# A half group's gathered results added late in the batch ahead of its own, and the first half of the values evacuated by ScalarE, in an attention stage that VectorE and TensorE share

## The chip, the cores and the metric

The kernel runs on one core of a Trainium2 chip. The metric is the time of one execution on the device, in microseconds (us). Before the change it is 1008.19 us, the median of 3 runs (1007.99 to 1009.01).

In what follows PE is TensorE, DVE is VectorE, ACT is ScalarE, POOL is GpSimd and SP is SyncE. PSUM is the memory that PE writes to, eight banks of 512 float32 columns on 128 partitions. SBUF is the working memory.

## The reference

The kernel computes a transformer of eight stages on `x` of shape (8, 256, 128): each stage adds, scaled by a gate, an attention or an expert network of the normed `x`. The change touches the seam of stages 2 and 3. Stage 2 is a network of experts that works on tokens sorted by expert, so each token's two results must be gathered back and added. Stage 3 is self-attention with 16 heads of 8 channels over the 256 tokens of a batch and 64 context tokens:

```python
x = x + jnp.tanh(g_ffn[0])   * _L0_ffn_ref(_layernorm(x), ...)          # stage 2: experts
x = x + jnp.tanh(g_xattn[1]) * _L1_xattn_ref(_layernorm(x), ctx, ...)   # stage 3: "Heads"
# stage 3, per batch of 256 tokens and per head:
#   P = softmax(q k^T / sqrt(8)) over 256 tokens + 64 context tokens;  out = (P v) W_proj + b_proj
```

Tokens of stage 3 must be normed, so a batch can be projected only once stage 2's results for it have been added to `x` and its statistics are known.

## The kernel before

Each engine runs its own list of instructions, in an order that the program writes out by hand. Engines meet only at semaphores. So the order on each engine is fixed, and what can change is who waits for whom.

The stage (class `HeadsStage`, lines 1160 to 1757) handles 8 batches. Its loop on PE, DVE and ACT runs through 10 rounds of 20 steps. In step n of round b:

- PE computes one bank of scores, 128 queries by 512 keys (L1385, or L1390 for the context keys in every fifth step), into one of three banks.
- DVE reduces that bank to row maxima (L1670). PE may not start the scores of step n before DVE has done step n - 3.
- PE computes, 16 steps behind, one bank of transposed scores (L1405, L1410), and ACT exponentiates it (L1590). PE may not be more than two such banks ahead of ACT.
- `extras(b, at)`, called with the step `at` from 0 to 19 on each of the three engines, adds the rest of the pipeline at fixed steps: for batch b + 1 the projection and the laying out of queries and keys, for batch b - 1 the products with the values, and for batch b - 2 the output projection and its addition to `x`.

The pieces that matter here:

- **The sums over values.** PE writes them for two groups of four heads into bank 5 (L1428, L1431, function `values`). When half a batch is complete, the bank is copied to the SBUF tile `AT` (L1691, function `evacuate`), PE transposes `AT` (L1440, function `turn_parts`), and DVE divides (L1677, L1684, function `take_parts`). The second half of batch b - 2 is copied at step 0 of round b, the first half of batch b - 1 at step 10. PE transposes at steps 1 and 11. Both copies are DVE's. The text calls them the **last copy** and the **first copy**. In the first copy the data are ready long before: PE writes them at steps 7 and 8.
- **The keys of the next batch.** DVE's masking copies (L1659, function `mask`) at steps 12 and 13 follow PE's transposes of the keys at step 11. PE's transposes of the second half of the queries (L1342, step 14) go into the same bank, so they wait for both masking copies. The text calls this point the **mask point** of a round.
- **The results of stage 2.** POOL gathers them from memory for each half group (256 tokens, the tokens of one batch) by indirect DMA (L997), four per half group. DVE adds them to `x` with four sums (L938, L940) and computes statistics (L154, L157), function `add_results`. POOL turns the statistics to a scale (L233, L236), and DVE norms at step 14 (L168). In round b, `add_results` for half group b + 2 stands at step 5, for b from 0 to 5. The text calls this block of eight DVE instructions the **added block**.
- **POOL** splits the queries and keys of batch b + 1 into bf16 parts during the first half of round b (L1218, L1226, L1231, L1233), then gathers the second pair of results of half group b + 3, then waits for PE (step 16) and splits the context keys of batch b + 2 (L1257, L1218, L1226 on 64 partitions), copies context values (L1269) and adds a bias (L1291).

Of the kernel before, what the change touches and what calls it, by code (L numbers as in the profile page):

```python
# [17 lines left out]
ACT = mybir.ActivationFunctionType  # L18
# [8 lines left out]
NG = NT // GROUP  # L27
# [91 lines left out]
class Norm:  # L119
# [122 lines left out]
    def act(self, a):  # L242
        self.turn.act(a)
# [916 lines left out]
class HeadsStage:  # L1160
# [379 lines left out]
    def act(self, a):  # L1540
        c, s = self.c, self.s
        bank = c.bank

        def split(b, k):
            a.wait_ge(s["qkv"], 2 * b + 1)
            if b:
                a.wait_ge(s["k_rows"], b)
            rows = bank[k][:, :].rearrange("p (i n h c) -> p n i h c", i=2, n=2, c=8)
            for n in range(2):
                a.activation(self.rest[:, n].rearrange("p (i h) c -> p i h c", i=2), rows[:, n], ACT.Copy,  # L1550
                             scale=1.0 if n else self.SCALE).then_inc(s["split"], 1)

        def split_values(b, k):
            a.wait_ge(s["qkv"], 2 * b + 2)
            if b >= 3:
                a.wait_ge(s["av"], 4 * (b - 2))
            a.activation(self.V[:, b % 3, :, 0:144].rearrange("p i (h c) -> p i h c", c=9)[:, :, :, 0:8],
                         bank[k][:, 0:2 * D].rearrange("p (i h c) -> p i h c", i=2, c=8), ACT.Copy) \
                .then_inc(s["split"], 1)

        def mask_context(b, k):
            a.wait_ge(s["k_t"], 3 * b + 2)
            for q in range(2):
                a.activation(self.KM[b % 2][:, q:16:2, S:S + SC],
                             bank[k].bitcast(BF16)[:, 0:512].rearrange("p (k t) -> p k t", t=SC), ACT.Copy,
                             scale=c.parity[:, q:q + 1]).then_inc(s["masked"], 1)

        def mask(b, g, q, k, done):
            a.wait_ge(s["k_t"], 3 * b + (3 if g else 1))
            a.activation(self.KM[b % 2][:, 8 * g + q:8 * g + 8:2, 0:S],  # L1570
                         bank[k].bitcast(BF16)[:, :].rearrange("p (k t) -> p k t", t=S), ACT.Copy,
                         scale=c.parity[:, q:q + 1]).then_inc(done, 1)

        def copy_again(b, g, k):
            a.wait_ge(s["q_top"], 2 * b + g + 1)
            a.activation(self.QE[:, 4 * g:4 * g + 4, :],  # L1576
                         bank[k].bitcast(BF16)[:, :].rearrange("p (k t) -> p k t", t=S), ACT.Copy) \
                .then_inc(s["q_again"], 1)

        def copy_out(b):  # L1580
            a.wait_ge(s["o_t"], b + 1)
            a.activation(self.OT, bank[6][:, 0:S], ACT.Copy).then_inc(s["o_turned"], 1)

        def exponentials(e):
            b, j, k = e // 20, e // 5 % 4, e % 5
            a.wait_ge(s["st"], e + 1)
            if 4 * b + j >= 2 and k in (0, 4):
                a.wait_ge(s["av"], 4 * b + j - 1)
            out = self.prob[(4 * j + k) % 8] if k < 4 else self.prob_c[:, j % 2, :]
            a.activation(out, bank[3 + e % 2][:, :], ACT.Exp).then_inc(s["exp"], 1)  # L1590

        def extras(b, at):
            ahead, behind, late = b + 1 < B, 0 <= b - 1 < B, 0 <= b - 2 < B
            if at == 2 and ahead:
                split(b + 1, 7)
            if at == 4:
                if ahead:
                    split_values(b + 1, 6)
                if behind:
                    copy_again(b - 1, 1, 7)  # L1600
            if at == 6 and late:
                copy_out(b - 2)
            if at == 14 and b < B:
                copy_again(b, 0, 6)
            if at == 17 and ahead:
                mask_context(b + 1, 6)
            if at == 19 and b + 2 < 2 * NG:
                turns.act_halves(a, b + 2, 1)
            if at in (18, 19) and ahead:
                mask(b + 1, 1, at - 18, 7, s["masked"])  # L1610

        turns = self.norm.turn
        turns.act_halves(a, 0, 1)
        a.wait_ge(s["ones_set"], 1)
        split(0, 0)
        split_values(0, 1)
        for q in range(2):
            mask(0, 0, q, 3, s["masked_v"])
        mask_context(0, 5)
        for q in range(2):  # L1620
            mask(0, 1, q, 4, s["masked"])
        turns.act_halves(a, 1, 1)
        for n in range(self.STEP * (B + 2)):
            if 0 <= n - self.LAG < self.STEP * B:
                exponentials(n - self.LAG)
            extras(n // self.STEP, n % self.STEP)

    def dve(self, v):
        c, s = self.c, self.s
        bank, own = c.bank, c.dve_chain  # L1630

        def next_stats(b):

            if b % 2 and self.next is not None:
                v.wait_ge(s["added"], 2 * b + 2)
                self.next.norm.stats(v, b // 2)

        def split_maxima(b, g, part):

            top, top_c = self.top[:, :, 8 * g:8 * g + 8], self.top_c[:, :, 8 * g:8 * g + 8]  # L1640
            rows = self.Q[b % 2][:, :, :, :].rearrange("p (i h) s c -> p i h (s c)", i=2)[:, :, 8 * g:8 * g + 8, :]
            if part == 0:
                v.wait_ge(s["maxed"], 20 * b + 10 * g + 10)
                own.link(v, v.tensor_tensor(top, top, top_c, ALU.min))
                own.link(v, v.tensor_copy(rows[:, :, :, 48], top))
                own.link(v, v.tensor_tensor(top, top, rows[:, :, :, 48], ALU.subtract))
            else:
                own.link(v, v.tensor_copy(rows[:, :, :, 49], top))
                own.link(v, v.tensor_tensor(top, top, rows[:, :, :, 49], ALU.subtract))
                v.tensor_copy(rows[:, :, :, 50], top).then_inc(s["top_rows"], 1)  # L1650
# [33 lines left out]
                v.tensor_tensor(self.O[:, :, at:at + 32].rearrange("p i (r k) -> p i r k", r=4), parts[:, :, :, 0:8],  # L1684
                                bc(rz[:, :, :, None], (P, 2, 4, 8)), ALU.mult).then_inc(s["heads"], 1)

        def evacuate(b, half):
            v.wait_ge(s["av"], 4 * b + 2 * half + 2)
            if b or half:
                v.wait_ge(s["parts"], 2 * b + half)  # L1690
            v.tensor_copy(self.AT, bank[5][:, :]).then_inc(s["evac"], 1)  # L1691

        def add(b):
            v.wait_ge(s["product"], b + 1)
            v.wait_ge(s["biased"], b + 1)
            for i in range(2):
                j = 2 * b + i
                v.scalar_tensor_tensor(c.X[:, j, :], bank[6][:, S + i * P:S + (i + 1) * P],
                                       c.gates[:, 1:2], c.X[:, j, :], ALU.mult, ALU.add).then_inc(s["added"], 1)

        def extras(b, at):
            ahead, behind, late = b + 1 < B, 0 <= b - 1 < B, 0 <= b - 2 < B
            if at == 0:
                if late:
                    evacuate(b - 2, 1)
                if behind:
                    split_maxima(b - 1, 1, 0)
            if at == 1 and behind:
                split_maxima(b - 1, 1, 1)
            if at == 2 and late:  # L1710
                take_parts(b - 2, 1)
            if at == 8 and late:
                add(b - 2)
            if at == 9 and ahead:
                copy_queries(b + 1, 0, 7)
            if at == 10:
                if behind:
                    evacuate(b - 1, 0)
                if b < B:
                    split_maxima(b, 0, 0)  # L1720
            if at == 11 and b < B:
                split_maxima(b, 0, 1)
            if at == 12:
                if behind:
                    take_parts(b - 1, 0)
                if ahead:
                    mask(b + 1, 0, 7)
            if at == 13 and ahead:
                mask(b + 1, 1, 7)
            if at == 15 and ahead:  # L1730
                copy_queries(b + 1, 1, 7)
            if at == 17 and 3 <= b - 2 < B - 1:
                next_stats(b - 2)
            if at == 14 and b == 5:
                next_stats(1)
            half = b + 2
            if half < 2 * NG:
                if at == 5:
                    self.before.add_results(v, half)
                if at == 14:  # L1740
                    self.norm.normalize(v, half // 2, half % 2)

        v.wait_ge(s["ones_set"], 1)
        v.wait_ge(s["split"], 1)
# [1570 lines left out]
```

## Time and profile before

| what | value |
|---|---|
| median of 3 runs | 1008.19 us (1007.99 to 1009.01) |
| the profiled execution: its own time | 1002.98 us |
| the profiled execution: span | 1001.3 us |
| PE, DVE, ACT, POOL busy | 79%, 65%, 38%, 37% of the span |
| mean granted clock of PE | 0.902 of full speed |
| the stage's steps in the trace | about 215 to 447 us |

The profiled execution is 5.21 us shorter than the median of the plain runs, so differences are worked out inside the trace and then applied to the median. A row of the timeline reads: start in us, duration in us, engine, line, operation, output and input, count, and in brackets the idle time of the engine just before, with what ended it. Consecutive instructions of one line are merged into one row; the last instruction of one row can overlap the first of the next by some hundredths, since the engines are pipelined.

Round b begins at step 0, whose last copy is easy to find in the trace. It starts at 270.31 us in round 2, 325.12 us in round 4, 352.52 us in round 5, 380.05 us in round 6 and 406.92 us in round 7. Rounds 2 to 4 are equal to 0.01 us.

### The profile page before, as it was taken

The numbers are of one execution on the slowest core, as the hardware profiler recorded it, in microseconds if no ns is written. First come the engines' busy times: TensorE is split into PE (matmuls) and PEld (weight loads), VectorE is DVE, ScalarE is ACT, GpSimd is POOL, SyncE is SP. The second block draws the span as 40 slices with busy tenths as digits, with TensorE's granted clock in tenths as the row PEclk, the third lists the DMA queues.
The fourth block names the chain that finished last, engine by engine and source line by source line (L and its number), as shares of the span: only waits on it lengthen the run. The fifth ranks groups of instructions, "written<-read, shape, count | busy, mean of one in ns | idle before, by whom it ended". The sixth has DMA issues, their size and how long they took to land.

```text
span 1001.3 us, 14752 instructions
## 1 busy us (share of the span) xinstructions
PE 791.5 (79%) x5059; PEld 540.7 (54%) x5059; DVE 650.8 (65%) x1844; ACT 376.6 (38%) x735; POOL 366.1 (37%) x502
## 2 busy tenths in 40 slices
PE   3635999646888888888989899888799879984374
PEld 1624888433444444433469666567343647774263
DVE  4774222366888888746977678996467458977421
ACT  2122444234666666751522564442200234441210
POOL 5234433276565535007745101102001015453353
PEclk9857999867999999998999899997899889995597
DMA  8605777200000000000000000000000230002210
GB/s 206 235 11 163 213 212 203 62 19 14 12 10 9 12 1 2 2 1 0 1 1 1 1 1 1 1 1 1 1 0 0 64 106 1 1 2 84 79 56 27
DMA packets 51772, 45.46 MB, mean 45 GB/s; under 512 B 6804, under 2 KB 47655, under 8 KB 51442
## 3 DMA queue, kind: packets, MB, share of 16 engines
q1 hardware_dynamic: 48146, 36.91, 12.5%
q0 software_dynamic: 3552, 7.61, 2.9%
q8 instruction: 41, 0.67, 0.3%
q14 instruction: 33, 0.27, 0.1%
HBM read 36.90 MB, written 7.80 MB: 45 GB/s over the span
## 4 chain that ended last, share of the span: by engine, by line
PE 53%; DVE 29%; issue 7%; POOL 4%; ACT 3%; DMA 3%; POOLq 0%; SPq 0%; DVEq 0%; ACTq 0%
PE psum L2473 6%; DVE scratch L1670 4%; PE psum L1131 4%; PE psum L2068 3%; PE psum L2747 3%; PE psum L2777 3%; DVE stats L154 3%; DVE XN L168 2%; PE psum L1428 2%; PE psum L610 2%; PE psum L277 2%; PE psum L1142 2%; DVE XN L1972 2%; PE psum L2113 2%; PE psum L2765 1%
## 5 line engine op out<-in xcount | busy, mean ns | idle before, releaser
L1670 DVE TENSOR_REDUCE scratch<-psum 128x2 f32<-128x512 f32 (+1 forms) x160 | 105.8, 683 | 35.3 <-PE psum L1390 19.3
L1590 ACT ACTIVATE scratch<-psum 128x512 f32<-128x512 f32 x160 | 93.9, 602 | 71.6 <-PE psum L1405 63.9
L233 POOL TENSOR_SCALAR veps<-moments 128x4 f32<-128x4 f32 (+1 forms) x48 | 10.4, 217 | 293.9 <-DVE moments L157 292.7
L277 PE MATMUL psum<-ident,XN 128*128 128x128 f32 x144 | 31.0, 352 | 44.8 <-DVE XN L168 41.2
L903 DVE SCALAR_TENSOR_TENSOR scratch<-psum,b_block_bias,scratch 128x256 f32<-128x256 f32 (+1 forms) x48 | 18.6, 430 | 71.9 <-ACT scratch L1056 64.0
L975 POOL DMA_INDIRECT scratch<-pair_rows,b_gather_at x39 | 39.3, 1007 | 68.6 <-PE psum L1104 41.8
L2473 PE MATMUL psum<-late,scratch 128*128 128x512 f32 x128 | 57.0, 607 | 5.7 <-DVE routing_wide L2416 5.0
L2679 POOL TENSOR_TENSOR scratch<-scratch,arena 128x1024 f32<-128x1024 f32 x16 | 30.4, 1902 | 76.9 <-DVE arena L2897 76.9
L1405 PE MATMUL psum<-scratch,arena 128*128 128x256 bf16 x256 | 49.3, 274 | 5.6 <-ACT scratch L1576 4.4
L292 ACT ACTIVATE XT<-psum 128x512 f32<-128x512 f32 (+1 forms) x40 | 22.2, 560 | 83.7 <-PE psum L277 83.6
L236 POOL TENSOR_TENSOR rstd<-veps,minus_half 128x4 f32<-128x4 f32 (+1 forms) x48 | 48.5, 1010 | 6.7 <-POOL veps L233 0.2
L277 PEld LDWEIGHTS psum<-ident,XN 128*128 128x128 f32 x144 | 21.3, 182 | 53.3 <-issue 25.9
L1385 PE MATMUL psum<-arena 128*128 128x512 bf16 x128 | 49.5, 393 | 0.6 <-DVE scratch L1670 0.6
L2473 PEld LDWEIGHTS psum<-late,scratch 128*128 128x128 f32 x128 | 24.8, 195 | 37.2 <-issue 30.5
L997 POOL DMA_INDIRECT arena<-pair_results,b_slot_bits x32 | 33.4, 1043 | 28.8 <-DMA pair_results<-scratch 21.0
L2427 DVE SCALAR_TENSOR_TENSOR X<-psum,routing_wide,X 128x128 f32<-128x128 f32 x128 | 33.8, 341 | 14.8 <-PE psum L2473 14.8
L1131 PE MATMUL psum<-scratch,arena 128*128 128x256 f32 (+1 forms) x192 | 39.5, 349 | 3.5 <-DVE scratch L903 2.8
L1972 DVE SCALAR_TENSOR_TENSOR XN<-psum,routing_wide,XN 128x128 f32<-128x128 f32 x128 | 35.4, 342 | 10.6 <-PE psum L2113 10.6
L2113 PEld LDWEIGHTS psum<-late,scratch 128*128 128x128 f32 x256 | 33.2, 191 | 16.3 <-issue 15.5
L1218 POOL CAST scratch<-scratch 64x384 bf16<-64x384 f32 (+3 forms) x64 | 32.3, 504 | 18.2 <-PE psum L1342 14.3
L168 DVE TENSOR_SCALAR XN<-X,moments,rstd 128x128 f32<-128x128 f32 x128 | 35.3, 338 | 5.3 <-POOL rstd L236 5.2
L1342 PE MATMUL psum<-ident,scratch 128*128 128x128 bf16 (+1 forms) x320 | 24.7, 224 | 16.0 <-POOL scratch L1277 7.5
(453 smaller groups left out, 2050.7 us busy)
## 6 DMA issues: line engine op xcount, KB each, us to landing
arena<-in_L_ffn_w SPq DMA_DIRECT2D x72, 128.0 KB
arena<-in_L_ffn_wg SPq DMA_DIRECT2D x24, 256.0 KB
wide<-in_L_xattn_Wkv SPq DMA_DIRECT2D x1, 2048.0 KB
wide<-in_L_ffn_W SPq DMA_DIRECT2D x1, 2048.0 KB, 8.8
late<-in_L_ffn_W SPq DMA_DIRECT2D x8, 256.0 KB, 6.9
pair_results<-scratch SPq DMA_DIRECT2D x15, 128.0 KB
X<-in_x SPq DMA_DIRECT2D x2, 512.0 KB, 5.0
C<-in_ctx SPq DMA_DIRECT2D x2, 512.0 KB, 6.8
```

What stands on the lines that cost most here:

```text
L168: v.tensor_scalar(self.dst[:, j, :], self.src[:, j, :], c.moments[:, j, 0:1], c.rstd[:, j:j + 1], ALU.subtract, ALU.mult).then_inc(c.norme ...
L236: g_.tensor_tensor(c.rstd[:, a:b], c.veps[:, a:b], c.minus_half[:, a:b], ALU.pow).then_inc(c.rstd_done, (b - a) // 2)
L277: last = t.transpose(c.bank[self.banks[g % 2]][:, i * P:(i + 1) * P], self.src[:, j, :], c.ident[:])
L975: g.indirect_dma_start(self.rows[:, u, i, :], None, self.given, bass.IndirectOffsetOnAxis(ap=self.gather_at[:, at:at + 1], axis=0), bounds ...
L1131: last = t.matmul(c.bank[4 + n % 2][:, k * self.SLOTS:k * self.SLOTS + rows], self.wg[:, n % self.RING, q, k * P:(k + 1) * P], self.z[:, n ...
L1385: last = t.matmul(out[:, 0:2 * S], queries[:, 4 * g + k, i * P:(i + 1) * P], keys[:, h:h + 2, 0:S], start=True, stop=True)
L1405: last = t.matmul(out[:, n * S:(n + 1) * S], keys[:, h, n * P:(n + 1) * P], self.QE[:, h // 2, :], start=True, stop=True)
L1590: a.activation(out, bank[3 + e % 2][:, :], ACT.Exp).then_inc(s["exp"], 1)
L1670: v.tensor_reduce(out, bank[m % 3][:, :].rearrange("p (h t) -> p h t", t=n), AX.X, ALU.max, negate=True).then_inc(s["maxed"], 1)
L1972: v.scalar_tensor_tensor(c.XN[:, j, :], c.bank[2 + n % 2][:, i * D:(i + 1) * D], one[:, j, e:e + 1], c.XN[:, j, :], ALU.mult, ALU.add) \
L2113: last = t.matmul(c.bank[2 + n % 2][:, i * D:(i + 1) * D], self.hidden[:, n % 2, i * P:(i + 1) * P], self.w2[:, e, :], start=True, stop=True)
L2473: last = t.matmul(c.bank[4 - 4 * (q % 2) + 2 * i + half][:, :], self.hidden[:, k, j * P:(j + 1) * P], self.w_down[:, k, half * 512:(half + ...
```

## The change

Two moves. First, `add_results` leaves step 5. Half group 2 stays there in round 0; half groups 3 to 7 are now added at step 17 of rounds 0 to 4, that is one round earlier and late in it. Normalization stays at step 14. Second, the first copy leaves DVE's step 10 and becomes an activation (L1588 in the new numbering) on ACT, at the same step, behind the exponentials of that step. The last copy stays with DVE. The number of copies, sums and statistics doesn't change.

```diff
 (ACT)
+        def evacuate_first(b):
+            a.wait_ge(s["av"], 4 * b + 2)
+            if b:
+                a.wait_ge(s["parts"], 2 * b)
+            a.activation(self.AT, bank[5][:, :], ACT.Copy).then_inc(s["evac"], 1)
...
+            if at == 10 and behind:
+                evacuate_first(b - 1)
 (DVE)
-        def evacuate(b, half):
-            v.wait_ge(s["av"], 4 * b + 2 * half + 2)
-            if b or half:
-                v.wait_ge(s["parts"], 2 * b + half)
+        def evacuate_last(b):
+            v.wait_ge(s["av"], 4 * b + 4)
+            v.wait_ge(s["parts"], 2 * b + 1)
             v.tensor_copy(self.AT, bank[5][:, :]).then_inc(s["evac"], 1)
...
-                if behind:
-                    evacuate(b - 1, 0)
...
+            if at == 5 and b == 0:
+                self.before.add_results(v, 2)
+            if at == 17 and b + 3 < 2 * NG:
+                self.before.add_results(v, b + 3)
             half = b + 2
-            if half < 2 * NG:
-                if at == 5:
-                    self.before.add_results(v, half)
-                if at == 14:
-                    self.norm.normalize(v, half // 2, half % 2)
+            if at == 14 and half < 2 * NG:
+                self.norm.normalize(v, half // 2, half % 2)
```

On DVE, in the kernel before, from the maxima of step 17 of round 1 to the first copy of round 2 (the maxima are L1670, the last and the first copy both L1691, the block L938 to L157):

```order
259 L1670 TENSOR_REDUCE scratch<-psum 128x2 x3
260 L1670 TENSOR_REDUCE scratch<-psum 128x8
261 L1670 TENSOR_REDUCE scratch<-psum 128x2
262 L1691 COPY scratch<-psum 128x512
...
274 L1670 TENSOR_REDUCE scratch<-psum 128x8
275 L1670 TENSOR_REDUCE scratch<-psum 128x2
276 L938 SCALAR_TENSOR_TENSOR X<-arena,routing_small,X 128x128
277 L940 SCALAR_TENSOR_TENSOR X<-arena,routing_small,X 128x128
...
286 L1670 TENSOR_REDUCE scratch<-psum 128x2
287 L1691 COPY scratch<-psum 128x512
```

The same place in the changed kernel, where the maxima are L1678 and the last copy is L1698:

```order
258 L1678 TENSOR_REDUCE scratch<-psum 128x2 x2
259 L938 SCALAR_TENSOR_TENSOR X<-arena,routing_small,X 128x128
260 L940 SCALAR_TENSOR_TENSOR X<-arena,routing_small,X 128x128
261 L938 SCALAR_TENSOR_TENSOR X<-arena,routing_small,X 128x128
262 L940 SCALAR_TENSOR_TENSOR X<-arena,routing_small,X 128x128
263 L154 BN_STATS stats<-X 128x6 x2
264 L157 BN_AGGR moments<-stats 128x2 x2
265 L1678 TENSOR_REDUCE scratch<-psum 128x2
266 L1678 TENSOR_REDUCE scratch<-psum 128x8
267 L1678 TENSOR_REDUCE scratch<-psum 128x2
268 L1698 COPY scratch<-psum 128x512
```

The block now stands three maxima ahead of the last copy, and neither the block nor the first copy stands between the last copy and the mask point any more.

On ACT, before, eight exponentials stand in a row in the middle of a round:

```order
121 L1590 ACTIVATE scratch<-psum 128x512 x2
122 L1582 ACTIVATE scratch<-psum 128x256
123 L1590 ACTIVATE scratch<-psum 128x512 x8
124 L1576 ACTIVATE scratch<-psum 128x1024
```

In the changed kernel the first copy (L1588) stands in the middle of the eight, which are L1596 there:

```order
123 L1596 ACTIVATE scratch<-psum 128x512 x2
124 L1582 ACTIVATE scratch<-psum 128x256
125 L1596 ACTIVATE scratch<-psum 128x512 x4
126 L1588 ACTIVATE scratch<-psum 128x512
127 L1596 ACTIVATE scratch<-psum 128x512 x4
128 L1576 ACTIVATE scratch<-psum 128x1024
```

The first copy is behind the exponentials of step 10 and ahead of those of step 11. The orders of PE and POOL are as before.

## Rows read from the trace of the kernel before

**Rows 1.** Windows of rounds 4 and 6, steps 0 to 10: length, busy by engine.

```profile
325.10:339.80 14.70, 12.59 (x124) 6.85 (x122) 12.68 (x32) 9.67 (x19) 9.48 (x17) 1.00 0.04 10
380.05:394.50 14.45, 12.44 (x123) 6.85 (x122) 9.96 (x25) 9.44 (x18) 7.24 (x15) 1.00 0.01 1
```

**Rows 2.** The copies' line L1691: who waited for it (us, times).

```profile
  PE psum L1440: 15.0, 15
```

**Rows 3.** Chain of what ended last, within round 4: start, us, what.

```profile
335.11 0.49 DVE stats L154 x2
...
339.90 0.60 DVE scratch L1691
...
345.42 0.62 PE psum L1342 x8
```

**Rows 4.** Timeline of DVE, round 4.

```profile
325.12 0.68 DVE L1691 COPY scratch<-psum 128x512 f32<-128x512 f32 x1
...
332.54 0.65 DVE L938 SCALAR_TENSOR_TENSOR X<-arena,routing_small,X 128x128 f32<-128x128 f32 x1
...
333.79 0.83 DVE L938 SCALAR_TENSOR_TENSOR X<-arena,routing_small,X 128x128 f32<-128x128 f32 x1
...
335.74 1.85 DVE L1670 TENSOR_REDUCE scratch<-psum 128x2 f32<-128x512 f32 x3
...
344.62 0.74 DVE L1659 TENSOR_SCALAR arena<-psum,parity 128x1024 bf16<-128x1024 bf16 x1
...
347.59 1.27 DVE L1670 TENSOR_REDUCE scratch<-psum 128x2 f32<-128x512 f32 x2
...
352.52 0.68 DVE L1691 COPY scratch<-psum 128x512 f32<-128x512 f32 x1
```

**Rows 5.** Timeline of PE, round 4, step 11.

```profile
340.64 0.63 PE L1440 MATMUL psum<-ident,scratch 128*128 128x128 f32 x4 [1.63 <-DVE scratch L1691]
```

**Rows 6.** Timeline of ACT, round 4, steps 9 to 11.

```profile
337.96 1.69 ACT L1590 ACTIVATE scratch<-psum 128x512 f32<-128x512 f32 x3 [0.97 <-PE psum L1405]
```

**Rows 7.** Timeline of DVE, round 6.

```profile
380.05 0.68 DVE L1691 COPY scratch<-psum 128x512 f32<-128x512 f32 x1
...
399.29 0.74 DVE L1659 TENSOR_SCALAR arena<-psum,parity 128x1024 bf16<-128x1024 bf16 x1
```

**Rows 8.** Timeline of POOL, round 4.

```profile
333.80 0.67 POOL L1233 TENSOR_TENSOR scratch<-scratch 128x256 f32<-128x256 f32 x1
...
348.66 0.42 POOL L1226 TENSOR_TENSOR scratch<-scratch 64x128 f32<-64x128 f32 x1
349.14 0.39 POOL L1218 CAST scratch<-scratch 64x256 bf16<-64x256 f32 x1
349.62 0.42 POOL L1226 TENSOR_TENSOR scratch<-scratch 64x128 f32<-64x128 f32 x1
350.10 0.28 POOL L1218 CAST scratch<-scratch 64x128 bf16<-64x128 f32 x1
```

**Rows 9.** The first sums' line L938: duration in ns min/median/max.

```profile
L938 DVE SCALAR_TENSOR_TENSOR X<-arena,routing_small,X x16: 339/648/835, 197.6 to 361.2; 128x128 f32<-128x128 f32 x16
```

**Rows 10.** Timeline of ACT, rounds 7 and 8, from step 9.

```profile
417.66 1.69 ACT L1590 ACTIVATE scratch<-psum 128x512 f32<-128x512 f32 x3 [0.52 <-PE psum L1405]
...
438.83 2.33 ACT L1590 ACTIVATE scratch<-psum 128x512 f32<-128x512 f32 x4 [0.30 <-PE psum L1405]
```

**Rows 11.** Timeline of PE, rounds 7 and 8, step 11.

```profile
419.48 0.63 PE L1440 MATMUL psum<-ident,scratch 128*128 128x128 f32 x4 [0.75 <-DVE scratch L1691]
...
439.72 0.60 PE L1440 MATMUL psum<-ident,scratch 128*128 128x128 f32 x4
```

**Rows 12.** Timeline of DVE, PE and POOL, end of round 0.

```profile
239.52 1.87 DVE L1670 TENSOR_REDUCE scratch<-psum 128x2 f32<-128x512 f32 x3
...
244.60 1.13 PE L1327 MATMUL psum<-c_Wqkv,XT 128*128 128x256 f32 x4 [0.88 <-ACT arena L1570]
...
239.10 0.28 POOL L1257 COPY scratch<-C 64x128 f32<-64x128 f32 x1 [2.25 <-PE psum L1342]
```

More of the change, by code:

```diff
@@ L1704, in extras @@
                 if late:
-                    evacuate(b - 2, 1)
+                    evacuate_last(b - 2)
                 if behind:
```

## Prediction

> **What bounds the stage now.** I read the page first, then windows of half rounds, the chain of what ended last inside one round, and then the timelines of DVE, PE, ACT and POOL around the three places that the change touches.
>
> In steps 0 to 10 of round 4, DVE is busy 12.68 us of 14.70 and PE 12.59, at the full clock. In round 6, which has no added block, DVE is busy only 9.96 us, yet the stretch still lasts 14.45 [rows 1]. So the block's 3.2 us (332.54 to 335.74) [rows 4] are mostly covered where they stand. PE would set the pace of that stretch without them.
>
> The chain inside round 4 shows two regimes. PE leads from the last copy to step 4. Then DVE leads through the block and the first copy up to the mask point. At 345.42 PE's transposes of the queries take over [rows 3], and PE leads up to step 19, when DVE's maxima and the last copy follow. The added block and the first copy both lie on the chain. PE waits 15.0 us in 15 waits for the copies of L1691 [rows 2]; in round 4 it stands idle 1.63 us before the transposes that follow the first copy [rows 5].
>
> I split a round at two points. E is the start of the last copy (325.12 in round 4, next at 352.52). M is the end of the second masking copy, 344.62 + 0.74 = 345.36. So E to M is 20.24 us and M to the next E is 7.16 us [rows 4].
>
> **E to M, rounds 1 to 5: about 0.86 us less each.** The block leaves this stretch, and so does the first copy. Round 6 shows what is left without the block: 399.29 + 0.74 - 380.05 = 19.98 us [rows 7]. The first copy is still in it and stands on the chain with 0.60 [rows 3], so DVE's way is 19.38 us, 0.86 less than 20.24.
>
> PE must be able to follow. ACT's three exponentials of steps 9 to 11 start at 337.96 and take 1.69, some 0.55 apart [rows 6]. The copy comes behind the second. It starts at 339.06, and as one more instruction of that size (128x512 float32 out of PSUM, 0.60 with its tail) it ends at 339.65. PE started its transposes 0.14 after the DVE copy's end (339.82 + 0.68 = 340.50, start 340.64 [rows 3, 5]), so it starts at 339.80 now: 0.84 earlier. PE also had about 0.17 of waiting left at M, by the same gap of issue, so 1.0 is there for PE and DVE's 0.86 decides. The exponentials of step 11 come 0.55 later; PE asks for them only at step 13, two banks on, so that is hidden.
>
> **M to the next E, rounds 1 to 4: about +0.36 us each.** This is where the block goes. Behind M, DVE works without a gap up to the end of step 17's maxima, 347.59 + 1.27 = 348.86 [rows 4], and then waits for PE in steps 18 and 19. The block starts at about 348.8. How long it lasts there is the unknown of this prediction; call it A.
>
> In its old place A is 3.2 us, though its sums can take 0.34 us each (the minimum) and not 0.65 (the median) [rows 9]. Round 4 shows why: the second L938 starts at 333.79 and ends at 334.62, 0.15 behind the end of POOL's 128x256 sum (333.80 + 0.67 = 334.47) [rows 4, 8]. A sum with two SBUF inputs stands until POOL's instruction is through. At the new place POOL is at work too, but with smaller instructions on 64 partitions, ending at 349.08, 349.53, 350.04 and 350.38 [rows 8].
>
> Ending each of the four sums either 0.34 after its start or 0.14 after the POOL instruction that runs, and starting the next a few hundredths on, I get ends at 349.22, 349.67, 349.93 to 350.18, and 350.31 to 350.56. From the last sum's end to the next maxima it takes 0.66 in the old place (statistics start at 335.11, a few hundredths behind the sum, and the maxima at 335.74 [rows 3, 4]), so the next maxima start at 350.97 to 351.22. I take A = 2.3, ending at 351.1. Then steps 18, 19 and 0 run back to back at 0.60, and the next E comes at 352.9. Before, it was 352.52 [rows 4]. The cover was DVE's idle time in steps 18 and 19; what the block needs beyond that cover is the +0.38, and I take 0.36 for A = 2.3 exactly (M + 7.52).
>
> The Trainium skill (SBUF — State Buffer, Who interferes with whom) speaks of an exclusive lock between a VectorE instruction with two SBUF inputs and a GpSimd one that reads SBUF: whoever starts first holds the port pair to its end. The pair of rows at 333.8 agrees in its 0.15 us. The rule speaks against this change, since the block is put among POOL's context-key work rather than into a quiet place. By the worst reading of it, all four sums wait out an instruction as long as the old ones.
>
> Bounds of A from rows: four sums near 0.34 and 0.66 of statistics give 2.0 us; four sums of 0.83, the largest [rows 9], give 4.0 us. My 2.3 is worked out from the POOL rows that really stand there.
>
> **Round 0: nothing.** The block starts there at about 240.7, behind the second of the maxima at 239.52. PE's projection for the next batch at 244.60 waits for ACT's mask [rows 12], not for DVE. Up to A = 2.55 this hides the block (240.7 + A + 0.60 for step 18, then some 0.75 of PE work to the projection); beyond that it costs A - 2.55. The gathers must have landed. POOL itself waits for them in its queue ahead of its copy at 239.10, so they have landed by then [rows 12], 1.6 us ahead of the block.
>
> **Rounds 5 to 8.** Round 5 gains 0.86 and has no block behind M; DVE sets its pace to the end, so it is kept. Round 6 never had a block: the copy's 0.60 goes, and PE's transposes come earlier by a like amount. Round 7 gains nothing: ACT's exponentials there start at 417.66, so the ACT copy would end at 417.66 + 2 x 0.55 + 0.60 = 419.35 and PE start at 419.49, where it starts at 419.48 now [rows 10, 11]. Round 8 loses. PE has no scores there and waits for ACT; at step 11 it starts its transposes at 439.72 without any wait for the copy. ACT's exponentials of steps 9 and 10 start at 438.83 and some 0.55 later, the copy runs from 439.93 to 440.50, PE starts at 440.63 [rows 10, 11]: +0.91 on the chain.
>
> **The sum.** Rounds 1 to 4: 4 x (-0.86 + 0.36) = -2.0. Round 5: -0.86. Round 6: -0.60. Round 8: +0.91. Together -2.55 us, and 4 x (A - 2.3) more for another A. The profiled execution would go from 1002.98 to about 1000.4. It lies 5.2 us under the median of the runs; the rounds of this stage run at the full clock [rows 1], so I apply the difference as it is: 1008.19 - 2.55 = 1005.6 us. What comes after the stage is moved, not changed. Differences below 0.2% (2.0 us) can't be told from no change here, and -2.55 is hardly over that.
>
> **Rivals.**
>
> 1. *The block stays expensive, but not ruinous* (A from 2.43 to 3.26). For it: 3.2 is what every block from round 1 on takes now. Against it: POOL's instructions at the new place are 0.28 to 0.42 us, not 0.67. With A = 3.2: +3.6, and 0.65 in round 0, in all +1.7, so 1009.9. With A = 2.8: -0.3, so 1007.9. Within 0.2%.
> 2. *ScalarE's copy comes no sooner than VectorE's.* Where ACT is late, PE gains only the 0.17 of its wait at M. For it: round 7. Against it: in rounds 2 to 5 the copy's slot (339.06) lies 0.76 ahead of DVE's (339.82). Then rounds 1 to 4 give 4 x (-0.17 + 0.36) = +0.8, round 5 -0.2, round 8 +0.9: +1.5, so 1009.7. Within 0.2%.
> 3. *Slower: the block at step 17 delays the last copy by more than the first half gives back.* Place: M to E of rounds 0 to 4. PE has nothing to do but wait for the last copy at step 1, so each 0.1 us of A costs 0.4 in rounds 1 to 4 and 0.1 in round 0. It decides from A = 3.26 (4 x 0.96 - 2.55 + 0.71 = +2.0). At the upper bound, 4.0, it is +6.8 - 2.55 + 1.45 = +5.7, so 1013.9. For it: the port conflict of rows 4 and 8, with a POOL instruction running nearly all the time from 348.66 to 350.38. Against it: none of these is long enough to hold a sum for 0.83.
> 4. *The gathers aren't landed at step 17*, so DVE waits and the block comes late, with the same price per 0.1 us. The POOL row of round 0 speaks against it. I give it the smallest chance.
>
> **Chances.** The forecast (A up to 2.43, ACT's copy on time) 0.52; rival 1: 0.26; rival 2: 0.12; rival 3: 0.07; rival 4: 0.03, half of it within 0.2%. So faster 0.52, within 0.2% 0.40, slower 0.08. The range: the lower bound A = 2.0 gives -3.75, 1004.4; executions differ from each other by about 1 us, so 1003.3 below. Above it reaches over most of rivals 1 and 2: 1009.5.
>
> **What would show it.** In the profile after: E to M of rounds 1 to 5 near 19.4 us instead of 20.24; PE's idle before L1440 at step 11 down from 1.63 to about 0.8, ended by ACT; M to E near 7.5 us in rounds 1 to 4 with no idle of DVE before steps 18 and 19; L938 and L940 shorter than 0.65 in the mean; E to E 26.9 instead of 27.40; round 8 longer by 0.9. Wrong if A is over 2.5, if PE is not earlier at step 11, if DVE waits for a DMA ahead of L938, or if PE turns out to have a wait of its own between steps 11 and 14 once the two are out of its way.

## The result, and the profile after

The changed kernel takes 999.72 us (median of 9 executions, 998.11 to 1002.09) against 1004.23 us for the kernel before (9 executions, 1002.18 to 1009.01). The ratio is 0.9947, 95% interval 0.9925 to 0.9969: faster by 0.53%. The forecast was faster, by 2.55 us, with 1005.6 us and a range of 1003.3 to 1009.5. The direction is right, the size is not, and the time lies below the range.

The profiled execution has a span of 997.3 us against 1001.3. Inside the stage the trace agrees with the working to about a tenth of a us per term. The rounds of the changed kernel can be read off the last copies and the second masking copies of round 4 (timeline of DVE; columns as in the rows of before; L1667 is the masking copy, L1698 the last copy, L1678 the maxima, L938 and L940 the four sums of the added block):

```profile
342.20 0.74 DVE L1667 TENSOR_SCALAR arena<-psum,parity 128x1024 bf16<-128x1024 bf16 x1
...
346.37 0.42 DVE L938 SCALAR_TENSOR_TENSOR X<-arena,routing_small,X 128x128 f32<-128x128 f32 x1
346.82 0.42 DVE L940 SCALAR_TENSOR_TENSOR X<-arena,routing_small,X 128x128 f32<-128x128 f32 x1
347.16 0.58 DVE L938 SCALAR_TENSOR_TENSOR X<-arena,routing_small,X 128x128 f32<-128x128 f32 x1
347.77 0.35 DVE L940 SCALAR_TENSOR_TENSOR X<-arena,routing_small,X 128x128 f32<-128x128 f32 x1
...
348.78 1.85 DVE L1678 TENSOR_REDUCE scratch<-psum 128x2 f32<-128x512 f32 x3
350.55 0.68 DVE L1698 COPY scratch<-psum 128x512 f32<-128x512 f32 x1
```

Round 4 begins here at 323.57. The mask point is 342.20 + 0.74 = 342.94, so E to M is 19.37 us, where it was 20.24 [rows 4] and 19.38 was worked out. M to the next E is 350.55 - 342.94 = 7.61, where it was 7.16 and 7.52 was worked out. The block lasts from 346.37 to 348.78, 2.41 us; the forecast took 2.3, the old place needs 3.2. DVE has no idle time in steps 18 and 19 any more.

POOL's timeline at that moment shows what holds the sums:

```profile
346.21 0.42 POOL L1226 TENSOR_TENSOR scratch<-scratch 64x128 f32<-64x128 f32 x1
346.69 0.39 POOL L1218 CAST scratch<-scratch 64x256 bf16<-64x256 f32 x1
347.17 0.42 POOL L1226 TENSOR_TENSOR scratch<-scratch 64x128 f32<-64x128 f32 x1
```

POOL's instructions end at 346.63, 347.08 and 347.59; DVE's first three sums end at 346.79, 347.24 and 347.74, each 0.15 to 0.16 later. The fourth, beside which POOL's instruction ends first, takes 0.35. In the old place the sums end the same 0.15 behind POOL's instructions, but these last 0.61 and 0.67 us ([rows 4, 8] show one such pair).

Step 11 of round 4, PE (answers to rows 5), and ACT with the copy L1588 behind two exponentials (answers to rows 6):

```profile
338.19 0.63 PE L1440 MATMUL psum<-ident,scratch 128*128 128x128 f32 x4 [0.73 <-ACT scratch L1588]
```

```profile
336.40 1.16 ACT L1596 ACTIVATE scratch<-psum 128x512 f32<-128x512 f32 x2 [0.97 <-PE psum L1405]
337.46 0.59 ACT L1588 ACTIVATE scratch<-psum 128x512 f32<-128x512 f32 x1
337.94 0.60 ACT L1596 ACTIVATE scratch<-psum 128x512 f32<-128x512 f32 x1
```

PE's wait is down from 1.63 to 0.73 us and ACT ends it. In round 8 the copy does harm, as worked out: PE now waits there (before, it didn't [rows 11]).

```profile
437.06 0.63 PE L1440 MATMUL psum<-ident,scratch 128*128 128x128 f32 x4 [0.67 <-ACT scratch L1588]
```

The whole stage, round by round, from the starts of the last copies (before 270.31, 297.72, 325.12, 352.52, 380.05, 406.92, 429.22, 445.50; after 269.61, 296.59, 323.57, 350.55, 377.21, 403.44, 425.72, 442.87) and the first maxima (215.85; 215.72):

| stretch | before | after | difference | worked out |
|---|---|---|---|---|
| first maxima to E of round 2 | 54.46 | 53.89 | -0.57 | -0.50 |
| rounds 2, 3, 4, each | 27.40 | 26.98 | -0.42 | -0.50 |
| round 5 | 27.53 | 26.66 | -0.87 | -0.86 |
| round 6 | 26.87 | 26.23 | -0.64 | -0.60 |
| round 7 | 22.30 | 22.28 | -0.02 | 0 |
| round 8, to the last copy | 16.28 | 17.15 | +0.87 | +0.91 |
| the stage | 229.65 | 227.15 | -2.50 | -2.55 |

How far one trace can be trusted here shows in six traces of the unchanged kernel (the one above and five of the experiments below). Their rounds 2 to 8 take 175.13 to 175.19 us, but the stretch ahead of round 2 takes 53.77 to 54.52, at mean granted clocks of 0.84 to 0.91. So the rounds can be compared to some hundredths and the first row of the table only to about 0.8 us. From round 2 on the change gives 1.93 us (175.19 to 173.26), where -2.05 was worked out. The -0.57 of the first row alone would show nothing.

So the stage does what was forecast. The rest of the 4.5 us of the medians comes from elsewhere: the experiments had to find out from where.

### The profile page after: what moved, and what is told of

Read it like the earlier page. It is cut to its first block, busy times and chain, and to the rows that moved or that the text cites. A ratio compares the mean times of both kernels' runs of the same rounds, so it can differ in the third digit from the quotient of the medians.

```text
span 997.3 us, 14752 instructions
## 1 busy us (share of the span) xinstructions
PE 789.4 (79%) x5059; PEld 540.1 (54%) x5059; DVE 644.4 (65%) x1836; ACT 380.2 (38%) x743; POOL 365.9 (37%) x502
## 3 DMA queue, kind: packets, MB, share of 16 engines
q0 software_dynamic: 3552, 7.61, 2.8%
## 4 chain that ended last, share of the span: by engine, by line
PE 51%; DVE 32%; issue 6%; POOL 4%; ACT 3%; DMA 2%; POOLq 0%; SPq 0%; DVEq 0%; ACTq 0%
PE psum L2479 6%; DVE scratch L1678 4%; PE psum L1131 4%; PE psum L2074 3%; PE psum L2753 3%; PE psum L2783 3%; DVE stats L154 2%; DVE XN L168 2%; PE psum L1428 2%; DVE scratch L1901 2%; PE psum L1114 2%; PE psum L610 2%; PE psum L277 2%; PE psum L1142 2%; PE psum L1405 2%
## 5 line engine op out<-in xcount | busy, mean ns | idle before, releaser
L1678 DVE TENSOR_REDUCE scratch<-psum 128x2 f32<-128x512 f32 (+1 forms) x160 | 106.3, 683 | 39.5 <-PE psum L1385 20.2
L1596 ACT ACTIVATE scratch<-psum 128x512 f32<-128x512 f32 x160 | 94.4, 602 | 65.9 <-PE psum L1405 65.8
L2119 PEld LDWEIGHTS psum<-late,scratch 128*128 128x128 f32 x256 | 33.2, 191 | 16.3 <-issue 15.5
```

The lines of the kernel that those rows point to most:

```text
L1678: v.tensor_reduce(out, bank[m % 3][:, :].rearrange("p (h t) -> p h t", t=n), AX.X, ALU.max, negate=True).then_inc(s["maxed"], 1)
```

## The experiments

"Stage" below is the time from the first maxima to the start of the last copy of round 9, and "rounds 2 to 8" the part of it from the last copy of round 2 on. The ratio is to the kernel before, on the same chip and beside it. Its interval reaches 2.2 to 3.2 us each way, so no ratio shows the fractions of a us that the last two columns show.

| run | what | median us | ratio, 95% interval | stage us | rounds 2 to 8 us |
|---|---|---|---|---|---|
| (the change) | both moves | 999.72 | 0.9947 [0.9925, 0.9969] | 227.15 | 173.26 |
| f1_after_again | both moves, again | 999.36 | 0.9934 [0.991, 0.9958] | 227.46 | 173.26 |
| e1_before_again | nothing | 1005.19 | 0.9997 [0.9967, 1.0027] | 229.65 | 175.13 |
| e2_copy_only | first copy on ACT | 1000.66 | 0.995 [0.9928, 0.9973] | 226.53 | 173.24 |
| e3_adds_only | block to step 17 | 1004.68 | 0.9985 [0.9958, 1.0011] | 230.05 | 175.51 |
| e4_copy_at_8 | both, copy at step 8 | 1004.25 | 0.9979 [0.995, 1.0008] | 225.73 | 171.47 |
| f3_copy_only_at_8 | first copy on ACT, at step 8 | 1003.51 | 0.9975 [0.9943, 1.0007] | 225.24 | 171.73 |
| f2_after_delayed | both, and four more reductions | 1003.56 | 0.9987 [0.9963, 1.0011] | 229.64 | 176.17 |
| f4_before_delayed | four more reductions | 1008.19 | 1.004 [1.001, 1.007] | 232.38 | 178.04 |

**Taking the change apart.** e2_copy_only is the changed kernel with the block back at step 5:

```diff
-            if at == 5 and b == 0:
-                self.before.add_results(v, 2)
-            if at == 17 and b + 3 < 2 * NG:
-                self.before.add_results(v, b + 3)
             half = b + 2
+            if at == 5 and half < 2 * NG:
+                self.before.add_results(v, half)
```

> Only the first copy moves to ScalarE; the added block stays at step 5 of rounds 0 to 5. Theory S, by the same chain: E to M in rounds 2 to 4 is 20.24 - 0.60 = 19.64 us, M to the next E stays 7.16, a round 26.80 instead of 27.40. Rounds 1 to 6 give 0.60 each, round 8 loses 0.9: the stage ends about 2.7 us earlier than before, 0.3 to 0.5 us earlier than with both moves. Rival (the block and the copy only pay together, since the block keeps VectorE late up to step 10): E to M stays within 0.2 us of 20.24 and the stage ends at most 1 us earlier.

Measured, in DVE's timeline of this run (last copies and the second masking copy of round 2):

```profile
268.10 0.68 DVE L1698 COPY scratch<-psum 128x512 f32<-128x512 f32 x1
...
287.21 0.74 DVE L1667 TENSOR_SCALAR arena<-psum,parity 128x1024 bf16<-128x1024 bf16 x1
...
295.00 0.68 DVE L1698 COPY scratch<-psum 128x512 f32<-128x512 f32 x1
```

E to M is 287.95 - 268.10 = 19.85, M to E 7.05, a round 26.90: 0.50 less than before instead of the expected 0.60. The stage is 3.1 us shorter (expected 2.7), and 0.6 us shorter than with both moves. But these 0.6 us lie ahead of round 2, where executions of one kernel differ by as much; from round 2 on the two kernels take 173.24 and 173.26. A round of rounds 2 to 4 costs 0.1 less without the adds' move, and round 5 costs 0.25 more. The rival is out: the copy's move pays alone.

e3_adds_only is the kernel before with this edit:

```diff
+            if at == 5 and b == 0:
+                self.before.add_results(v, 2)
+            if at == 17 and b + 3 < 2 * NG:
+                self.before.add_results(v, b + 3)
             half = b + 2
-            if half < 2 * NG:
-                if at == 5:
-                    self.before.add_results(v, half)
```

> Only the added block moves to step 17 of the round ahead; both copies stay with VectorE. Theory S: E to M is 19.98 us as in round 6 (0.26 less), M to the next E is 7.6 (0.45 more) as in the changed kernel, a round 27.6: slower than before by 0.2 us in rounds 1 to 4, faster by 0.26 in round 5, in all 0.5 us slower. Rival (the block's 3.2 us were on the chain, so taking it out of the first half gives what the chain showed): E to M near 17 to 18 us, a round under 26.

```profile
270.54 0.68 DVE L1691 COPY scratch<-psum 128x512 f32<-128x512 f32 x1
...
289.82 0.74 DVE L1659 TENSOR_SCALAR arena<-psum,parity 128x1024 bf16<-128x1024 bf16 x1
...
298.14 0.68 DVE L1691 COPY scratch<-psum 128x512 f32<-128x512 f32 x1
```

E to M is 290.56 - 270.54 = 20.02, M to E 7.58, a round 27.60. Rounds 2 to 8 are 0.3 us longer than before, and the stage 0.4 (expected 0.5). 3.2 us of DVE work taken out of the chain of steps 5 to 15 gave 0.22 us there, and cost 0.42 where it was put. PE sets the pace right behind it: DVE's idle time between E and M grows from 1.71 us (round 3 of the kernel before) to 4.22 us (round 2 here), and all of it ends with PE's scores. Of the two moves only the copy's gains anything in the stage.

**The copy two steps earlier.** e4_copy_at_8 is the changed kernel, f3_copy_only_at_8 is e2_copy_only, both with

```diff
-            if at == 10 and behind:
+            if at == 8 and behind:
                 evacuate_first(b - 1)
```

> The changed kernel, but ScalarE makes the first copy at step 8, right behind the values it copies, not behind the exponentials of step 10. Theory S: in rounds 1 to 6 VectorE decides, so E to M stays 19.38; in round 7 TensorE's transposes come 0.7 us earlier, in round 8 they lose only about 0.2 us instead of 0.9. The stage ends 1.4 us earlier than in the changed kernel. Rival (ScalarE still decides the pace between steps 11 and 14): E to M of rounds 2 to 4 falls too, to about 18.6, and the stage ends 5 us or more earlier.

> Only the first copy moves to ScalarE, at step 8; the added block stays at step 5. Theory S: rounds 2 to 4 last 26.89 us as with the copy at step 10 alone (VectorE decides), rounds 7 and 8 give 0.7 us each more, and the stage from the first maxima to the last copy of round 9 is 226.5 - 1.5 = 225.1 us, the shortest of all. Total 4.5 us under the kernel before. Rival (without the late block, the copy at step 8 lets TensorE ahead and the maxima follow earlier): rounds 2 to 4 below 26.5 us.

PE's timeline of e4_copy_at_8, rounds 4 and 7 at step 11:

```profile
340.16 0.60 PE L1440 MATMUL psum<-ident,scratch 128*128 128x128 f32 x4
...
417.81 0.60 PE L1440 MATMUL psum<-ident,scratch 128*128 128x128 f32 x4
```

PE waits for no copy there any more. E to M of rounds 2 to 4 stays 19.38 all the same (299.54 to 318.18 + 0.74), so DVE decides there, as forecast. Rounds 7 and 8 give 0.81 and 0.67, and the stage is 1.4 us shorter than with the copy at step 10 (1.8 from round 2 on). f3_copy_only_at_8 has rounds of 26.89 and a stage of 225.24, the shortest of all, 4.4 us under the kernel before; from round 2 on it is e4_copy_at_8 that is shortest, by 0.26.

Yet neither shows this in its total: 1004.25 and 1003.51, with single executions from 998.81 to 1006.79 and from 996.28 to 1008.34. The changed kernel, with a longer stage, had all 21 of its executions between 997.79 and 1002.09.

**The kernel before against itself, and the changed one again.**

> The kernel before, unchanged, timed against itself. Theory S (the change is worth what its stage shows, 2.3 to 2.6 us, and the rest of the measured 4.5 us is the spread of the clock grants in the stages behind it): the ratio is 1 within about 0.2%, and this execution's stages behind the last copy of round 9 (555.8 us in the first profile) last between 554 and 558 us, with differences of 1 us or more to the first profile in single stretches. Theory D (the change itself makes the later stages about 1.4 us shorter): they last 555.8 within 0.3 us, since nothing is changed.

> The changed kernel once more. Theory S (only the stage's 2.5 us are the change's, the rest is the spread of executions): its stage from the first maxima to the last copy of round 9 is 227.2 us again, against 229.7 before, and the ratio lies between 0.995 and 1.0, nearer to 0.9975 than the first 0.9947. Theory D (the change also speeds up what comes behind): 0.9945 again, and the stages behind the last copy are 1 us or more shorter than in the unchanged kernel's second profile.

The kernel before repeats its ratio of 1 and its stage. What follows the last copy of round 9 takes 555.6 us, where the first profile has 555.8, as theory D of e1_before_again expected; in the changed kernel's two traces it takes 554.4 and 554.5. The changed kernel repeats its 0.53% and more (0.66%), so that is not the luck of a few executions, and the reading that only 2.5 us were real becomes unlikely for the total: 2.5 us would be a ratio of 0.9975, above both intervals. Laid side by side, the executions show what differs. For those listed here the mean granted clock is on record:

| kernel | executions | with clock 0.890 or less | their median us | median of the others us |
|---|---|---|---|---|
| before | 82 | 24 | 1009.9 | 1003.2 |
| changed | 21 | 0 | | 999.5 |
| e2_copy_only | 12 | 0 | | 1000.7 |
| e3_adds_only | 12 | 1 | 1004.9 | 1004.5 |
| f2_after_delayed | 12 | 1 | 1006.8 | 1003.4 |
| f4_before_delayed | 12 | 5 | 1013.2 | 1006.3 |
| e4_copy_at_8 | 12 | 5 | 1005.9 | 1002.4 |
| f3_copy_only_at_8 | 12 | 7 | 1005.6 | 1000.0 |

(The expectation of g1_before below says 79 and 1003.3 for the kernel before; the record holds 82 such executions, with 24 in the lower kind all the same.) About three executions in ten of the kernel before are of a kind with a lower clock and some 6.7 us more: the 24 take 1006.64 to 1012.28 us, the 58 others 1000.87 to 1006.13. The first three, from which the 1008.19 came, have the times of that kind, though their clocks aren't on record; the profiled one, at clock 0.902, is of the other. The changed kernel had none in 21. For the variants the same limit of 0.890 doesn't part the times so cleanly: the seven of f3_copy_only_at_8 run from 997.50 to 1008.34.

**Does the moment at which the later stages begin decide it?** f2_after_delayed (and f4_before_delayed in the same way on the kernel before) puts the stage's end back:

```diff
+            if b == B - 1:
+                for _ in range(4):
+                    own.link(v, v.tensor_reduce(self.top[:, 0, 0:2], bank[0][:, :].rearrange("p (h t) -> p h t", t=S),
+                                                AX.X, ALU.max, negate=True))
             v.tensor_copy(self.AT, bank[5][:, :]).then_inc(s["evac"], 1)
```

> The changed kernel with four more reductions of a PSUM bank on VectorE ahead of the last copy of round 9 (their result isn't used), which put the stage's end back by some 2.9 us, to 0.3 us behind that of the kernel before. Theory S: 2.9 us slower than the changed kernel, and the same as the kernel before within 1 us. Theory D, if the later stages are faster by what they find when they start (a shorter rest of some other engine, another moment): the later stages keep their gain only if it does not hang on the moment of the start; then it stays 1.5 to 2.5 us under the kernel before.

> The kernel before with the same four reductions ahead of the last copy of round 9. Theory S: 2.9 us slower than the kernel before, in the trace and, within its interval, in the total. Theory D: the total moves by something clearly other than 2.9 us (none, or 5 and more), since the moment at which the later stages begin decides on their clock.

The four reductions take 2.87 us in both traces, and rounds 2 to 8 are 2.9 us longer than without them. The whole stages came to 229.64 and 232.38 us, 2.2 to 2.5 and 2.7 more. The delayed changed kernel is 1003.56, 4.1 us over the changed one and level with the kernel before, although it has only 1 of 12 executions of the lower kind. The delayed kernel before is 1008.19, 4.2 to 4.6 us over its neighbours, with 5 of 12. By the medians a delay of 2.9 us cost about 4 in both, but the intervals of the ratios (0.2 to 0.3% each way) reach down to the delay's own size, so theory S is refuted for neither. The share of the lower kind, 1 of 12, lies between 0 of 21 and 24 of 82, too few executions to tell. These two runs neither show nor exclude that the moment decides; the traces of the next part speak against it.

**Where the lower kind loses its time.** Four more traces of the unchanged kernel before, without rounds:

> The kernel before, for one more trace, unchanged as the three that follow. Of 79 executions of it so far, 24 had a mean granted clock of 0.890 or less and a median of 1009.9 us, the others 1003.3 us; of the changed kernel's 21 none had. The profiles so far all come from the upper clock. With four more, the chance to see one of the slow kind is about 3 in 4. Theory H (the slow kind arises in the stage of the change): its extra time and lower clock lie between 215 and 447 us. Theory B (it arises behind the stage): the stage takes 229.7 us as ever, and the extra time lies in the stages behind it.

> As the run before it: theory H, extra time inside the stage; theory B, the stage takes 229.7 us and the extra time lies behind it, in stretches that differ in the granted clock alone.

> As the two runs before it: theory H, extra time inside the stage; theory B, the stage takes 229.7 us and the extra time lies behind it, in stretches that differ in the granted clock alone.

> As the three runs before it: theory H, extra time inside the stage; theory B, the stage takes 229.7 us and the extra time lies behind it, in stretches that differ in the granted clock alone.

They were taken on another chip than the experiments above. Their clocks are 0.896, 0.893, 0.887 and 0.896, their times 1003.56, 1005.58, 1009.87 and 1001.27 us; g3_before is of the lower kind. Its stage takes 228.91 us, no longer than the 229.15 to 229.68 of the other three, so theory B holds. The extra time lies behind it, between the last copy of round 9 and the first value products of the last attention stage (L2777 in the kernel before). The table splits this at three instructions: the last output product of stage 4's attention (L2074), and the first and the last sum of its experts' results (L1972). Each number is that of one execution.

| trace | the whole, to L2777 | to L2074 | to the first L1972 | to the last L1972 | to L2777 | mean granted clock |
|---|---|---|---|---|---|---|
| before; e1, g1, g2, g4 | 382.1 to 382.5 | 100.7 to 101.0 | 31.8 to 32.1 | 58.5 to 58.6 | 190.8 to 191.1 | 0.91 to 0.92 |
| g3_before (lower kind) | 389.2 | 101.0 | 33.2 | 58.5 | 196.5 | 0.89 |
| changed; f1 | 381.4, 381.5 | 100.1, 100.2 | 29.5 | 58.5 | 193.3 | 0.92 |
| f2_after_delayed | 382.1 | 100.8 | 32.0 | 58.5 | 190.8 | 0.91 |
| f4_before_delayed | 383.1 | 101.3 | 32.0 | 58.5 | 191.3 | 0.90 |
| e2_copy_only | 385.1 | 100.7 | 29.4 | 58.6 | 196.4 | 0.90 |
| e3_adds_only | 385.0 | 100.7 | 29.4 | 58.6 | 196.3 | 0.90 |
| e4_copy_at_8, f3 | 386.7, 386.8 | 101.1 | 33.2 | 58.5, 58.6 | 193.9 | 0.89 |

One trace need not stand for its kernel: that of e2_copy_only has the lowest clock of its twelve executions (0.891, where ten of them have 0.899 or more).

Windows over the second and the fourth of these pieces (columns: length; busy us of PE, its weight loads, DVE, ACT, POOL with counts; granted clock; share of the DMA engines; GB/s), for the kernel before:

```profile
546.20:578.30 32.10, 27.78 (x135) 18.88 (x134) 21.25 (x83) 16.83 (x38) 5.77 (x7) 0.89 0.00 1
636.80:827.60 190.80, 161.58 (x636) 100.24 (x635) 125.94 (x434) 43.74 (x73) 22.40 (x33) 0.89 0.08 23
```

g3_before:

```profile
546.60:579.80 33.20, 28.86 (x135) 19.94 (x135) 21.30 (x83) 16.84 (x38) 5.78 (x7) 0.85 0.00 0
638.30:834.80 196.50, 168.69 (x636) 104.55 (x635) 126.46 (x434) 43.71 (x73) 23.22 (x33) 0.84 0.08 22
```

and the changed kernel:

```profile
543.00:572.50 29.50, 24.76 (x135) 17.09 (x135) 21.29 (x83) 16.84 (x38) 5.78 (x7) 1.00 0.00 1
631.00:824.30 193.30, 164.33 (x636) 102.38 (x635) 126.34 (x434) 43.76 (x73) 22.43 (x33) 0.88 0.08 22
```

The work is the same, 135 and 636 matmuls with the same counts on the other engines. DVE's and ACT's busy times hardly differ, while PE's grow as the granted clock falls. These clocks are means over a clock that stands at one of two levels, 2.4 GHz (1.00) or 1.2 GHz: between 561 and 567 us of the kernel before it is at the lower one.

```profile
561.00:567.00 6.00, 5.84 (x15) 3.23 (x14) 3.05 (x11) 0.38 (x2) 0.00 (x0) 0.50 0.00 0
```

In the second piece, at the start of stage 4's experts, the changed kernel has the full clock throughout and gains 2.6 us on the kernel before, after 0.6 in the first piece. In the fourth it loses 2.5 again, and it ends 0.7 to 1.0 us ahead at L2777. Of the 7.1 us that g3_before loses on the kernel before, 1.1 are in the second piece and 5.7 in the fourth. Where the lower level falls matters too, and not only how much of it there is: e1 has a mean of 0.87 in the fourth piece and takes 191.1 us, the changed kernel has 0.88 and takes 193.3.

Neither the program nor the moment at which the stage ends, counted from the start of the execution, decides alone on the grants. The last copy of round 9 starts at 445.50 us in the first profile, at 445.60 in g3_before and at 445.97 in g1_before, with the same instructions before and after, and what follows up to L2777 takes 382.1, 389.2 and 382.4 us.

## Why the prediction was right in the stage and wrong in the total

- *The stage.* From round 2 on all terms of the sum hold within 0.1 us: rounds 2 to 4 -0.42 each for -0.50, and so on in the table above. A was 2.41 for 2.3, and M to the next E grew by 0.45 for 0.36. That the whole stage came to -2.50 for -2.55 is in part luck, for 0.57 of it lie ahead of round 2; by the second trace of the changed kernel the stage is 2.19 shorter. "The rounds of this stage run at the full clock [rows 1]" was read from rounds 4 and 6 and holds from round 2 on (1.00), not ahead of it (0.91 in the profile before). That a sum ends 0.15 us behind POOL's instruction was read from one pair of rows and held in three more; the Trainium skill's lock (SBUF — State Buffer, Who interferes with whom) agrees with them. Its warning was right in kind and small in size, since the instructions it waits for are short ones there.
- *Rivals.* ACT's copy came in time (rival 2 is out in rounds 1 to 6 and holds in round 7). No gather was late (DVE shows no wait for a DMA ahead of L938 in these rounds). A stayed under 2.43, narrowly.
- *The two moves.* The forecast took them as one sum and didn't notice from its own terms that the adds' move loses: 0.26 off E to M and 0.36 on M to E. e3_adds_only shows it (0.22 off, 0.42 on), and beside the copy's move it loses too, by e2_copy_only: 0.48 off and 0.56 on. The copy's move doesn't need it.
- *The step that failed* is "What comes after the stage is moved, not changed", and with it "I apply the difference as it is: 1008.19 - 2.55". Two parts of it were wrong. The median of three, 1008.19, belonged to a kernel whose executions come in two kinds, at about 1003.2 and 1009.9 us; over the later executions its median is 1004.0. This alone put the forecast 4 us too high, and "executions differ from each other by about 1 us", read from the same three, made the range too narrow: the 82 spread over 11 us. And the later stages did not stay as they were: none of the changed kernel's 21 executions was of the lower-clock kind, against 24 of 82, and its two traces are shorter behind the stage. Counting it out for the mean of the executions: 24 of 82 times 6.7 us is 2.0, the stage gives 2.5, what is behind it 0.7 to 1.0 in the traces, together 5.2 to 5.5. The means differ by 5.8 us in the first comparison and 5.5 in the second. Within the upper kind the medians differ by 3.7 us (1003.2 and 999.5), for 3.2 to 3.5 by the traces. The warning was in the profile's own time, 5.2 us under the median of the runs: the text named this gap and passed over it.
- *What stays open* is why the grants differ behind the stage. Shown is that they do, where, and by how much. With the changed kernel's end put back, the stretch L2074 to L1972 is 32.0 us again, as in the kernel before, but e3_adds_only ends its stage 0.55 us later than the kernel before (446.05 for 445.50) and still has the full clock there, and g3_before ends it at the same moment as the kernel before and gets less. What PE did ahead of each grant was not varied alone, so no cause is named. That the change lowers the share of the lower kind rests on the counts, 0 of 21 against 24 of 82; why it does is not shown.

## What to carry to other kernels

Work a change out between two points that recur on the chain (here the last copy and the mask point), and check each part with a round that lacks it: round 6 gave E to M to 0.01 us before anything ran. Work on the chain of one engine is worth only what the other engine lets it be worth; 3.2 us taken off gave 0.2. To tell variants apart by single traces, compare a stretch that repeats in several traces of the unchanged kernel. Before a time is forecast in absolute terms, compare the profiled execution's own time with the runs: here a gap of 0.5% was the sign that executions come in kinds, and a change of 0.25% in one stage came with another share of each kind.

## What the runs showed of the hardware that was not expected

- A kernel's executions on one core can fall into two kinds by the granted clock of PE (0.883 to 0.890 and 0.893 to 0.903), 6.7 us apart of 1004, with 24 of 82 in the lower one. Between kernels that differ in one stage alone, the executions at 0.890 or less range from 0 of 21 to 7 of 12; in the traces most of what that costs lies in stages that the edit doesn't touch (g3_before, 7.1 us).
- The same 135 matmuls, with the same work beside them, took 29.5 us at a granted clock of 1.00, 32.1 at 0.89 and 33.2 at 0.85.
- The shortest stage (225.24 us, f3_copy_only_at_8) didn't give the shortest kernel: in its trace the 1.9 us that it won on the changed kernel (1.5 from round 2 on) were lost behind it, 386.8 us for 381.4.
- The start of the stage itself moves by up to 3.9 us between executions of the same instructions (first maxima at 214.60 in g4_before, 218.47 in g2_before), and the stage keeps its length to 0.8 us through that (228.91 to 229.68 in six traces). This start makes up 3.9 of the 4.3 us between those two executions (1001.27 and 1005.58 us).
